# First gate of a macaron block: logits in four column groups, part of the normalising on GpSimd, top-k for two batches at once

## What is computed

```python
x = L0_attn_x                                    # (8, 1024, 512) float32
x = x + 0.5 * ffn(layernorm(x))                  # expert-choice mixture, 32 experts
x = x + attn(layernorm(x))                       # linear attention, 16 heads
x = x + 0.5 * ffn(layernorm(x))

def ffn(x):                                      # E=32, D=512, H=2048, K=8
    logits = einsum('bsd,ed->bse', x, gate_w) + gate_b
    probs  = softmax(logits, axis=-2)            # over the 1024 tokens
    vals, idx = top_k of probs over the tokens, 8 for each (batch, expert)
    merged = sum over the 8 of vals * x[idx]     # (b, e, d)
    h = gelu([merged, 1] @ w1[e])                # (513, 2048) for each expert
    o = [h, 1] @ w2[e]                           # (2049, 512) for each expert
    return scatter-add of o * vals to the 8 tokens
```

## Time and profile before

| | |
|---|---|
| median of 3 runs | 2429.77 us (2426.45 to 2435.95) |
| profiled execution, own time | 2426.14 us |
| its span, first to last instruction | 2424.4 us |
| busy: PE, DVE, ACT, POOL | 2084.9, 753.8, 813.6, 600.5 us |
| moved by DMA | 762.22 MB, mean 314 GB/s |
| mean granted TensorE clock | 0.940 of 2.4 GHz |

### The profile page before, as it was taken

One profiled execution on the slowest core, in us unless ns is written; L12 is line 12 of the kernel. 1 busy time (PEld: TensorE's weight loads), 2 busy tenths in 40 slices (PEclk: granted clock), 3 DMA queues, 4 the chain that ended last, 5 costly groups with the idle time before them and its releaser, 6 DMA issues.

```text
span 2424.4 us, 44443 instructions
## 1 busy us (share of the span) xinstructions
PE 2084.9 (86%) x18836; PEld 1194.9 (49%) x18836; DVE 753.8 (31%) x1272; ACT 813.6 (34%) x1449; POOL 600.5 (25%) x755
## 2 busy tenths in 40 slices
PE   6979999999999999979999999999776666666565
PEld 3435665665665665756666666676521111111111
DVE  6841111111111111256776777677420000000002
ACT  6731211111111111257777777777500000000000
POOL 2210000000000000067777777777411000000002
PEclk9999999999999999989999999999987888887887
DMA  9849999999999999654544445444399999999994
GB/s 359 323 164 390 400 409 397 406 406 394 409 404 398 398 417 407 227 203 152 160 148 152 154 148 169 143 160 144 129 390 423 424 425 424 424 424 425 425 424 196
DMA packets 130661, 762.22 MB, mean 314 GB/s; under 512 B 21108, under 2 KB 21108, under 8 KB 77216
## 3 DMA queue, kind: packets, MB, share of 16 engines
q1 hardware_dynamic: 118688, 701.35, 73.9%
q10 hardware_dynamic: 9216, 50.34, 5.0%
q0 software_dynamic: 2560, 7.70, 0.8%
HBM read 648.09 MB, written 105.91 MB: 311 GB/s over the span
## 4 chain that ended last, share of the span: by engine, by line
PE 51%; DMA 34%; POOL 6%; ACT 3%; issue 3%; DVE 2%; SPq 0%; POOLq 0%; ACTq 0%; DVEq 0%
PE ps L272 46%; DMA big<-in_L_ffn_w 32%; PE ps L276 3%; POOL s L1260 1%; POOL big L1257 1%; DMA big<-in_L_attn_x 1%; POOL big L1231 1%; POOL big L1262 1%; DMA big<-xt_scratch 1%; ACT big L1100 1%; DMA xt_scratch<-big 1%; ACT ps L1084 1%; PE ps L646 1%; ACT big L1095 0%; POOL big L1224 0%
## 5 line engine op out<-in xcount | busy, mean ns | idle before, releaser
L272 PE MATMUL ps<-big 128*32 128x512 f32 (+6 forms) x13904 | 1074.4, 427 | 225.1 <-DMA big<-in_L_ffn_w 209.7
L272 PEld LDWEIGHTS ps<-big 128*32 128x32 f32 (+3 forms) x13904 | 398.2, 127 | 818.1 <-issue 477.8
L280 DVE TENSOR_TENSOR big<-ps,big 128x512 f32<-128x512 f32 (+3 forms) x309 | 319.7, 1066 | 177.6 <-PE ps L272 177.6
L272 PE MATMUL ps<-wth,xth 128*128 128x512 f32 x768 | 309.5, 403 | 4.7 <-ACT big L811 4.7
L688 ACT ACTIVATE big<-ps 128x512 f32<-128x512 f32 x64 | 38.3, 598 | 806.2 <-PE ps L272 806.2
L272 PE MATMUL ps<-wth,xtl 128*128 128x512 f32 x768 | 300.3, 391 | 0.0
L272 PE MATMUL ps<-wtl,xth 128*128 128x512 f32 x768 | 299.8, 390 | 0.0
L1249 POOL TENSOR_SCALAR big<-big 128x1 f32<-128x1 f32 x64 | 12.2, 190 | 897.8 <-ACT ps L1084 892.1
L272 PE MATMUL ps<-wo,s 128*128 128x512 f32 x768 | 210.5, 409 | 3.4 <-ACT big L1148 1.9
L712 DVE COPY big<-ps 128x128 f32<-128x128 f32 x64 | 18.4, 287 | 589.1 <-PE ps L646 589.1
L276 PE MATMUL ps<-big 128*128 128x128 f32 x1032 | 161.0, 289 | 30.4 <-ACT big L489 15.5
(11 more groups left out here) (112 smaller groups left out, 1826.3 us busy)
## 6 DMA issues: line engine op xcount, KB each, us to landing
big<-in_L_ffn_w SPq DMA_DIRECT2D x256, 2048.0 KB, 24.2
p_scratch<-big ACTq DMA_DIRECT2D x64, 768.0 KB, 10.3
big<-p_scratch SPq DMA_DIRECT2D x64, 768.0 KB, 5.4
big<-in_L_attn_x SPq DMA_DIRECT2D x16, 1024.0 KB, 13.1
xt_scratch<-big SPq DMA_DIRECT2D x16, 1024.0 KB, 11.4
big<-xt_scratch SPq DMA_DIRECT2D x16, 1024.0 KB, 16.7
big<-in_L_attn_x SPq DMA_DIRECT2D x64, 256.0 KB, 3.1
x_weight_scratch<-big SPq DMA_DIRECT2D x64, 256.0 KB, 3.3
```

What stands on the lines that cost most here:

```text
L272: return nc.tensor.matmul(o, l, r, start=start, stop=stop, skip_group_check=True)
L280: return nc.vector.tensor_tensor(o, p, q, op)
```

## The change

The first gate is written anew, and the work at its end is placed elsewhere. Logits: sixteen matmuls of 128 columns, the four tiles of a group into four blocks of 32 PSUM partitions, and four small bias copies on ACT in place of one. Normalising: POOL does tiles 0 to 2 of each group, ACT tile 3; `NMG` and `STD` are made on POOL, `STD` by a multiplication instead of a power. All `XT4` copies are on ACT. Top-k runs in rounds: batches 0 and 1, 2 and 3, 4 and 5 together on 64 partitions, 6 and 7 alone; the exponential goes to a buffer of its own (`LE`), and `MT` has two buffers in this gate. x has 14 buffers (four of them in ring slots 2 and 3), its first group is loaded tile by tile, 7 loads are given out ahead and one more behind each store. Only chunks 0 and 1 are loaded within the gate, at groups 10 and 12. The first two `weights_pe` steps run within the gate's end, six after expert 0's first layer, eight after its gelu transposes, in four PSUM banks instead of two. `ahead_pe(0)` runs at the end of expert 0, tiles 2e-1 and 2e in expert e, and tile 63 alone after expert 31. Where a semaphore counted 8 batches of top-k it counts 5 rounds (`NR`).

```diff
@@ buffers
-        XLA = [at(p, 2048).rearrange("p (t d) -> p t d", t=4) for p in (*range(w_at, m_at, 2048), os_at, os_at + 2048)]
+        XLA = [at(p, 2048).rearrange("p (t d) -> p t d", t=4) for p in (
+            xg_at, xg_at + 2048, *range(w_at, xg_at, 2048), os_at, os_at + 2048, *range(2 * SLOT, w_at, 2048))]
+        ROUNDS = [(0, 2), (2, 4), (4, 6), (6, 7), (7, 8)]
...
+        def round_dve(dve, r):
+            R_, half = rows(r)
+            W = M[0][R_, half, :]
+            dve.wait_ge(s_L4, 8 * ROUNDS[r][1])
+            nc.vector.max(T8[R_, :], L[0][R_, :]).then_inc(s_top, 1)
+            dve.wait_ge(s_top, 4 * r + 1)
+            nc.vector.tensor_scalar(NMX[R_, :], T8[R_, 0:1], -1.0, None, ALU.mult).then_inc(s_top, 1)
+            nc.vector.match_replace(W, T8[R_, :], L[0][R_, :], LOWEST).then_inc(s_top, 1)
+            dve.wait_ge(s_top, 4 * r + 3)
+            tt(W, L[0][R_, :], W, ALU.not_equal).then_inc(s_top, 1)
+        def round_act(act, r):
+            act.wait_ge(s_top, 4 * r + 2)
+            act.wait_ge(s_wt, r - 1)
+            nc.scalar.activation(LE[R_, :], L[0][R_, :], ACT.Exp, bias=NMX[R_, :], accum_out=SUM[R_, :]).then_inc(s_exp, 1)
+        def round_weights(dve, r):
+            R_, half = rows(r)
+            W = M[0][R_, half, :]
+            dve.wait_ge(s_exp, r + 1)
+            nc.vector.reciprocal(RSUM[R_, :], SUM[R_, :]).then_inc(s_rsum, 1)
+            dve.wait_ge(s_rsum, r + 1)
+            dve.wait_ge(s_top, 4 * r + 4)
+            nc.vector.scalar_tensor_tensor(out=W, in0=LE[R_, :], scalar=RSUM[R_, :], in1=W, op0=ALU.mult,
                                            op1=ALU.mult).then_inc(s_wt, 1)
...
@@ gate_sp
+            for g in range(NG):
+                sp.wait_ge(s_xt4, 4 * g + 4)
+                sp.dma_start(xtd[g], XT4[g % 3]).then_inc(d_xts[g % 3], 16)
+                if g + 7 < NX4:
+                    load_x(g + 7)
+                if g + 7 in (NX4, NX4 + 1):
+                    sp.wait_ge(s_mtok, 1)
+                    load_x(g + 7)
+                if g == 9:
+                    load_biases(sp)
+                if g in (10, 12):
+                    load_chunk(sp, (g - 10) // 2)
...
@@ gate_pe
+        def logits_pe(pe, h):
+            pe.wait_ge(s_xt4, 4 * h + 4)
+            pe.wait_ge(s_L4, 4 * h)
+            for k in range(4):
+                for j in range(4):
+                    t = mm(ps[32 * j:32 * j + 32, 4, 0:128], GT[:, k, :], XT4[h % 3][:, k, 128 * j:128 * j + 128],
+                           k == 0, k == 3)
+            t.then_inc(s_lg4, 1)
...
+            for g in range(NG):
...
+                transposes_pe(pe, g)
+                if g:
+                    logits_pe(pe, g - 1)
+                for b in first(g, 4) + second(g, 5):
+                    pe.wait_ge(s_pr3, b)
                     merge_tokens_pe(pe, b, 6)
+            logits_pe(pe, NG - 1)
+            merge_end_pe(pe, 4, 7)
+            merge_tokens_pe(pe, 5, 6)
+            merge_transpose_pe(pe, 6, 5)
+            merge_end_pe(pe, 5, 0)
+            merge_tokens_pe(pe, 6, 6)
+            weights_pe(pe, 0, 1)
+            merge_transpose_pe(pe, 7, 5)
+            weights_pe(pe, 1, 2)
+            merge_tokens_pe(pe, 7, 6)
+            merge_end_pe(pe, 6, 1)
+            merge_end_pe(pe, 7, 7)
...
@@ gate_act
+            for g in range(NG):
+                for i, j in enumerate((3, 0, 1, 2)):
+                    act.wait_ge(s_tp4, 4 * g + i + 1)
+                    act.wait_ge(s_lg4, g - 2)
+                    act.wait_ge(d_xts[g % 3], 16 * (g // 3))
+                    nc.scalar.copy(XT4[g % 3][:, :, 128 * j:128 * j + 128],
+                                   ps[:, j, :].rearrange("p (k t) -> p k t", k=4)).then_inc(s_xt4, 1)
+                    if i == 0 and g + 1 < NG:
+                        normalise_act(act, g + 1)
+                    if i == 1:
+                        for b in first(g, 4) + second(g, 4):
+                            merge_transpose_act(act, b, 5 + b % 2 * 2)
+                        for r in ended(g, 3):
+                            round_act(act, r)
+                if g:
+                    logits_act(act, g - 1)
+                for b in first(g, 4) + second(g, 5):
                     merge_tokens_act(act, b, 6)
+            logits_act(act, NG - 1)
+            merge_tokens_act(act, 5, 6)
+            round_act(act, 3)
+            merge_transpose_act(act, 6, 5)
+            round_act(act, 4)
+            merge_tokens_act(act, 6, 6)
+            weights_act(act, 0, 1)
+            merge_transpose_act(act, 7, 5)
+            weights_act(act, 1, 2)
+            merge_tokens_act(act, 7, 6)
...
@@ gate_dve
+                for r in ended(g, 2):
+                    round_dve(dve, r)
+            round_weights(dve, 3)
+            round_dve(dve, 4)
+            merge_end_dve(dve, 4, 7)
+            merge_end_dve(dve, 5, 0)
+            round_weights(dve, 4)
+            weights_dve(dve, 0, 1)
+            merge_end_dve(dve, 6, 1)
+            weights_dve(dve, 1, 2)
+            merge_end_dve(dve, 7, 7)
...
@@ gate_pool
+                nc.gpsimd.tensor_tensor(RS_, VEG[g % 4], NHALF.broadcast_to([128, 4]), ALU.pow).then_inc(s_rs4, 1)
+                nc.gpsimd.tensor_scalar(NMG[g % 4], MV_[:, 3, 0:1], RS_[:, 3:4], -1.0, ALU.mult, ALU.mult)
+                for j in range(3):
+                    nc.gpsimd.tensor_scalar(X[:, j, :], X[:, j, :], MV_[:, j, 0:1], RS_[:, j:j + 1], ALU.subtract,
+                                            ALU.mult).then_inc(s_nmp, 1)
+                nc.gpsimd.tensor_tensor(STD[:, 4 * g:4 * g + 4], VEG[g % 4], RS_, ALU.mult).then_inc(s_std, 1)
...
@@ load_weight
             if m < 2:
-                sp.wait_ge(s_mg, 8)
-                sp.wait_ge(s_bk, 1)
+                sp.wait_ge(s_mtok, 5)
             else:
                 sp.wait_ge(s_wT, 4 * m - 4)
...
@@ load_xg
-            sp.wait_ge(s_mtok, 4)
+            sp.wait_ge(s_mtok, 8)
...
@@ experts_sp
                 load_weight(sp, 0)
+                sp.wait_ge(s_mtok, 6)
+                load_chunk(sp, 2)
+                sp.wait_ge(s_mtok, 7)
+                load_chunk(sp, 3)
                 load_weight(sp, 1)
+                load_weight(sp, 2)
                 load_xg(sp, 0)
+                load_weight(sp, 3)
                 load_xg(sp, 1)
-                load_weight(sp, 2)
-                load_weight(sp, 3)
...
@@ experts_pe
+                if p == 0 and e == 0:
+                    weights_pe(pe, 2, 8)
                 if p == 0 and e:
-                    ahead_pe(pe, 2 * e - 2)
+                    ahead_pe(pe, 2 * e - 1)
...
+                if p == 0 and e == 0:
+                    weights_pe(pe, 8, 16)
+                    bias_pe(pe)
                 if p == 0 and e:
-                    ahead_pe(pe, 2 * e - 1)
+                    ahead_pe(pe, 2 * e)
...
                 if p == 0 and e == 0:
-                    weights_pe(pe)
+                    ahead_pe(pe, 0)
-            if p == 0:
-                ahead_pe(pe, NT - 2)
             scatter_pe(pe, p, 7)
             if p == 0:
                 ahead_pe(pe, NT - 1)
```

More of the change, by code:

```diff
@@ L141, in macaron_block @@
         PR = B1
+        WB = (2, 3, 6, 7)
         g1 = Area(oc_at)
@@ L237, in macaron_block @@
             turn[g] = turns[slot_of(g)]
[L240 to L244, removed]
+        ROUNDS = [(0, 2), (2, 4), (4, 6), (6, 7), (7, 8)]
+        NR = len(ROUNDS)
+        round_of = {b: r for r, (lo, hi) in enumerate(ROUNDS) for b in range(lo, hi)}
         def kvs(n):
@@ L262, in h4, with ended, first, second @@
             return t.rearrange("p (g n) -> p g n", g=4)
-        def batch(g, after):
-            b = (g - after) // 2
-            return [b] if (g - after) % 2 == 0 and 0 <= b < B else []
+        def ended(g, after):
+            return [r for r, (lo, hi) in enumerate(ROUNDS) if 2 * hi - 1 + after == g]
+        def first(g, after):
+            return [ROUNDS[r][0] for r in ended(g, after)]
+        def second(g, after):
+            return [ROUNDS[r][1] - 1 for r in ended(g, after) if ROUNDS[r][1] - ROUNDS[r][0] == 2]
         def load_done(g):
-            return d_xg[g % NX4], 16 * (g // NX4 + 1)
+            return d_xg[g % 7], 16 * (g // 7 + 1)
         def mm(o, l, r, start, stop):
@@ L420, in gate_sp @@
-            for g in range(NX4):
+            for g in range(4, 7):
                 load_x(g)
-                if g == 3:
-                    load_biases(sp)
[L424 to L433, removed]
-                if 1 <= g <= 4:
-                    load_chunk(sp, g - 1)
+            for g in range(NG):
[7 more added lines that the diff above has]
+                if g == 9:
+                    load_biases(sp)
+                if g in (10, 12):
+                    load_chunk(sp, (g - 10) // 2)
@@ new lines, in gate_pe, with logits_act @@
+            pe.wait_ge(s_mg, 5)
+            merge_end_pe(pe, 7, 7)
+        def logits_act(act, h):
```

(27 more changed lines are left out.)

261 lines of the change are left out of this document (118 added, 143 removed).

## The result

| | before | after |
|---|---|---|
| median | 2428.11 us, 4 runs | 2518.9 us, 4 runs |
| ratio to before | | 1.0396 (95% interval 1.0376 to 1.0417) |
| profiled span | 2424.4 us | 2512.5 us |
| mean granted clock | 0.940 | 0.921 |

A forecast was written before the change was run, and what follows sets the result against it. The gate was taken as bound by PE and its partners, the expert pass by transfers. Gate and transfers 36.5 us plus 7.6 at the pass's end gave 44 us: 2386 us against the median 2429.8, range 2372 to 2405.

The forecast's parts named there:

- POOL's term: Gate: each normalising instruction on POOL takes 0.9 us, POOL 4.7 us a group, 5.3 with DVE's meetings.
- one at 1.28 us a tile: Gate: rival with POOL needing 6.4 us a group, meetings included; 16 us more, 2402; chance 0.13.
- the slower one: Gate: rival that POOL's `tensor_scalar` runs far under the `affine_select` rate; gain gone at 2.1 us a tile; chance 0.06.
- The first copy: Gate's start: with x loaded in tiles of 256 KB, the first copy comes at about 9.5 us.
- Both early waits go: Gate: the 14.3 us wait for an `XT4` store and the 18.7 us wait for an x load disappear.
- The tail: Gate's end behind the last `XT4` copy: about 21.5 us against 24.5; expert 0 starts at 118.5.
- Meetings of DVE and POOL: Gate: DVE's two-input instructions hold POOL back, at worst 0.6 us a group.
- the clock falls: Gate: rival that half of it runs at the lower clock level; plus 20 us, 2406; chance 0.08.
- Expert 0: First expert: PE's work ends 2.7 us later with one more tile done; Wo lands near 17.5 us after its start.
- this 2.5 counts: First expert: chunks 8 and 9 land at 49 instead of about 51.5 us, a 2.5 us gain replacing PE's 2.7.
- The pass: Expert pass: transfer-bound, mean 25.7 to 25.9 us an expert; one more store costs 2 us.
- End of the pass: After expert 31: one tile leaves, minus 8.4 us, less 0.6 for ACT's uncovered `PT` copy: minus 7.6 us.

The follow-up runs named there:

- dve_one: reload_early with one of POOL's three normalising instructions a group (tile 2) done by DVE; 2407.2 us, ratio 0.9932.
- dve_two: reload_early with two of POOL's three normalising instructions a group (tiles 1 and 2) done by DVE; 2397.9 us, ratio 0.9901.
- reload_early: The changed kernel with the reload of `xt_scratch` issued one expert sooner, at the end of expert 2h-2 instead of 2h-1; 2428.3 us, ratio 1.0011.
- order_early: The kernel before with the new order of the ahead tiles and the reloads one expert earlier; 2425.4 us, ratio 1.0007.
- dve_two_order: dve_two with the old order of the ahead tiles and the old place of the reloads; 2396.8 us, ratio 0.9891.
- order_only: The kernel before with the new order of the ahead tiles alone, reloads in their old places; 2521.7 us, ratio 1.0408.
- order_undone: The changed kernel with the old order of the ahead tiles, everything else as changed; 2426.4 us, ratio 1.0016.

## Why the prediction was wrong, step by step

**Gate, POOL's term.** "It has one input, so I take 0.9": 2.08 us. The bound "0.6 and 1.28" was no bound, since no row had `tensor_scalar` at this size, and a row of another operation was taken to cap it. (0.550 us for 284 columns is also 0.99 at the same rate for 512, not 0.9; that is small beside the rest.) The group became 7.69 us where 5.4 stood. Two rivals had POOL as the pace, one at 1.28 us a tile, and the slower one with this mechanism, but with a chance of 0.06. Its turning point of 2.1 us a tile fits the measured 2.08 partly by luck: it set 1.95 us a group for POOL's other work, which took 1.45 (7.69 - 3 x 2.08), and it weighed the gain of the whole change. The gate's own gain of 36 us is used up by the longer group alone, 16 x (7.69 - 5.4) = 37, and gelu 0 came at +2.5. dve_one and dve_two confirm the cause.

**Gate, the other terms.** The first copy starts at 11.94, forecast 9.5. With POOL relieved a group takes 5.8 us on the mean ((104.84 - 11.97) / 16 in dve_two, from the start of its first copy), forecast 5.4, and 6.5 where the rounds run (PE's weight transposes of two rounds start at 47.87 and 73.78, four groups apart). "Both early waits go" holds in the changed kernel, whose chain is POOL; in dve_two, with POOL relieved, two stores of 10.40 and 12.05 us are in the chain again. ACT's logits copies are 0.36 us each, not 0.28; PE's sixteen products 1.08 us in the shortest rows, inside 0.9 to 1.9. The tail was right within 1.1 us: last copy to expert 0 22.6 us (134.6 to 157.2), forecast 21.5.

**Meetings of DVE and POOL.** Forecast at most 0.6 us a group. All 48 normalising instructions lie between 2.065 and 2.163 us, so they stretched POOL's long instruction by 0.1 us at most. Short work shows more: DVE's weights rose from 1.28 to 1.43 and 1.52 in single rounds of the tail, and POOL's power from a mean of 1.03 to 1.24 us in dve_two, where DVE normalises beside it. That it is the meeting which costs this is likely, not tested.

**Clock.** The gate's granted clock fell from 0.97 to 0.89 (77 to 137 us), with PE busy 0.69 of it. In reload_early, the same program up to expert 0, it was 0.77 in the profiled execution. While POOL is the pace this hardly shows (last `XT4` copy at 134.6 and 135.9). In the tail it does; the last sixteen token products, first in the chain of the changed kernel, then in that of reload_early:

```profile
152.22 1.89 PE ps L280 x16
```

```profile
154.40 3.44 PE ps L280 x16
```

Expert 0 starts at 157.2 and 160.9, 2.4 us of it behind the last copy. So a lower clock goes with 3.7 us here, and gelu 0 differs by that much (163.45 and 167.19) with nothing in the code to make it. The rival "the clock falls" had 20 us; a small part of it came true, also in dve_two, where the transposes behind PE's wait took 3.61 us.

**Expert 0.** Forecast 34.5 us from gelu 0 to gelu 1, measured 36.2 in the changed kernel (39.4 for the same code in reload_early, where one stretch of PE's work in it, forty products, takes 9.04 us in place of 7.27). PE's wait for Wo ends 18.2 us after expert 0's start, assumed 17.5; that is less than half of the difference. But the credit behind it ("this 2.5 counts") was wrong in sign: order_early and dve_two_order show that PE's extra tile is paid in full. That the ring of four chunks, which lets transfers run ahead by one expert only, is the reason was read from the code and not tested.

**The pass.** Here the step that failed was never written: the prediction moved `ahead_pe` by one tile and counted its matmuls and its store, but put its reload at nothing. Tile 4h is split while tile 4h-1 is projected. Before, that was the second of expert 2h's tiles; now it is the first. SP issues the reload at the end of expert 2h-1 in both. The slack of half an expert was the cover; it cost 89 us when it went, some 6 us for each of 14 reloads. reload_early, order_only and order_undone show it from three sides. Nothing in the windows would have warned: the wait of ACT for `xt_scratch`, 81.0 us in 14 waits up to 8.6 us, stood in the list of waits of the kernel before, harmless as long as half an expert of PE's work covered it.

**End of the pass.** Right: -7.5 us for -7.6.

## What to carry to other kernels

When work is moved within a software pipeline, list what each moved step consumes, and compare the queue position of the transfer that brings it with the new time of need; a wait that is long and harmless before is the first to become a bound. Never cap an unknown price by another operation of the same engine: move one instruction first and read its row, above all on GpSimd. And a pass that is held by transfers need not hide PE work: here a tile cost its full time in the first expert as at the end, probably because the ring was full.

## What the hardware showed that was not expected

GpSimd's `tensor_scalar` on 128x512 float32 takes 2.08 us with two operations, 1.64 with one, while its `tensor_tensor` takes 1.28 and VectorE does the two operations in 0.54. The same `tensor_scalar` on 128x1 takes 0.27. Sixteen products of 128 columns into four column groups take 1.08 us in the shortest rows, against 3.55 for the same logits in one group. In dve_two, behind a wait of 4.3 us for VectorE, PE's sixteen transposes took 3.61 us at a granted clock of 0.50, against 1.91 at full clock.
